# Scan stage of an eight-stage kernel: where the expert mix and the product delta · xs are computed

## The reference

```python
xc = _silu(xc + conv_b[None, :, None])               # after a causal convolution with 4 taps
dt_lo, Bm, Cm = ...                                  # three slices of x_ld @ x_proj_w.T
delta = jax.nn.softplus(dt_lo @ dt_proj_w.T + dt_proj_b)
def step(h, inp):                                    # h: 512 channels x 16 states
    dA = jnp.exp(d_t[:, :, None] * negA[None])
    h = dA * h + (d_t * x_t)[:, :, None] * B_t[:, None, :]
    y_t = jnp.einsum('bdn,bn->bd', h, C_t)
y = (y + x_ld * D[None, None, :]) * _silu(z_bld)
out = y @ out_proj_w.T
```

## Time and profile before

| | before |
|---|---|
| runs | 2511.66, 2512.00, 2514.43 us; median 2512.0 |
| profiled execution | 2519.74 us, its span 2518.0 us |
| scan stage, first scan to end of the last | 1255.3 to 1758.6 us |
| PE, DVE, ACT, POOL busy over the span | 88, 66, 58, 35 per cent |
| mean granted PE clock | 0.938 of full speed |

### The profile page before, as it was taken

One profiled execution on the slowest core, in us unless ns is written; L12 is line 12 of the kernel. 1 busy time (PEld: TensorE's weight loads), 2 busy tenths in 40 slices (PEclk: granted clock), 3 DMA queues, 4 the chain that ended last, 5 costly groups with the idle time before them and its releaser, 6 DMA issues. The chain is left out here.

```text
span 2518.0 us, 47690 instructions
## 1 busy us (share of the span) xinstructions
PE 2217.8 (88%) x16425; PEld 1937.2 (77%) x16425; DVE 1674.2 (66%) x4020; ACT 1453.1 (58%) x3815; POOL 889.7 (35%) x906
## 2 busy tenths in 40 slices
PE   6887979999999979998489999999686899996997
PEld 4776968999999959997266676677685576766997
DVE  5785767888888846554498898777464554554554
ACT  5674547777777723333487777775342566663342
POOL 3221240011111120000678887667485233332000
PEclk8897989999999979999699999999897999997999
DMA  4000120000000463333311111000400000000001
GB/s 151 1 1 17 35 68 18 2 18 18 18 18 18 144 197 119 120 111 94 129 41 51 51 50 47 35 35 1 119 1 1 1 1 1 1 1 1 1 1 34
DMA packets 74371, 111.77 MB, mean 44 GB/s; under 512 B 16174, under 2 KB 59814, under 8 KB 73016
## 3 DMA queue, kind: packets, MB, share of 16 engines
q1 hardware_dynamic: 66648, 87.23, 10.7%
q0 software_dynamic: 7488, 21.50, 2.6%
HBM read 79.73 MB, written 28.97 MB: 43 GB/s over the span
## 5 line engine op out<-in xcount | busy, mean ns | idle before, releaser
L2064 POOL TENSOR_TENSOR l2a_hb<-l2a_hb,l2a_Cb 128x1024 f32<-128x1024 f32 x128 | 302.8, 2377 | 107.7 <-DVE l2a_hb L2551 106.5
L2551 DVE TENSOR_TENSOR_SCAN l2a_hb<-l2a_dA,l2a_dB 128x1024 f32<-128x1024 f32 x128 | 288.8, 2275 | 31.4 <-PE l2a_dB L2158 26.1
L2158 PE MATMUL l2a_dB<-l2a_diag,l2a_dxT 64*128 64x128 f32 x2048 | 190.1, 306 | 38.8 <-DVE l2a_hb L2551 25.9
L2158 PEld LDWEIGHTS l2a_dB<-l2a_diag,l2a_dxT 64*128 64x128 f32 x2048 | 139.9, 194 | 104.0 <-PE l2a_dB L2158 37.2
L2388 ACT ACTIVATE l2a_dA<-l2a_delta,l2a_An 128x255 f32<-128x255 f32 x512 | 213.4, 498 | 6.9 <-DVE l2a_hb L2551 6.7
L964 PE MATMUL l1a_QK<-l1a_xh,early_wqkv_h 128*128 128x256 f32 x512 | 147.1, 287 | 1.5 <-DVE l1a_xl L128 1.5
L964 PE MATMUL l1a_QK<-l1a_xh,early_wqkv 128*128 128x256 f32 x512 | 144.6, 282 | 0.0
L964 PE MATMUL l1a_QK<-l1a_xl,early_wqkv_h 128*128 128x256 f32 x512 | 144.3, 282 | 0.0
L2178 PE MATMUL l2a_YS<-ident,l2a_hb 128*128 128x128 f32 x1024 | 142.2, 285 | 1.0 <-POOL l2a_hb L2064 1.0
L1240 ACT ACTIVATE l1a_ex<-l1a_S,l1a_nm 128x256 f32<-128x256 f32 x256 | 119.3, 471 | 36.5 <-DVE l1a_nm L1292 35.1
L2178 PEld LDWEIGHTS l2a_YS<-ident,l2a_hb 128*128 128x128 f32 x1024 | 116.5, 145 | 12.2 <-POOL l2a_hb L2064 1.3
(11 more groups left out here) (767 smaller groups left out, 7812.4 us busy)
## 6 DMA issues: line engine op xcount, KB each, us to landing
l2a_Cb<-c_rows SPq DMA_DIRECT2D x8, 2048.0 KB
l1f_xl<-moe_x_rows SPq DMA_DIRECT2D x95, 128.0 KB
moe_y_rows<-l1f_yo SPq DMA_DIRECT2D x95, 128.0 KB, 1.7
first_raw<-in_L_attn_w_qkv_dram SPq DMA_DIRECT2D x18, 256.0 KB, 2.8
moe_x_rows<-X SPq DMA_DIRECT2D x1, 4224.0 KB, 17.2
l1f_dL<-in_L_ffn_Wd_dram SPq DMA_DIRECT2D x1, 3072.0 KB
X<-in_L_attn_x_dram SPq DMA_DIRECT2D x8, 256.0 KB, 6.0
routes_raw<-in_L_attn_w_o_dram SPq DMA_DIRECT2D x4, 512.0 KB
```

Of the source, the lines that this page charges most:

```text
L2064: nc.gpsimd.tensor_tensor(h[:, :, :], h[:, :, :], Cb[p][:, s0:s0 + UN, :], ALU.mult).then_inc(hc_ready, 1)
L2158: last = nc.tensor.matmul(out[:, m:m + 2, j * P + a:j * P + a + HP], dxT[q][a:a + HP, j, c * P:(c + 1) * P], diag[q][a:a + HP, j, s0 + m:s ...
L2551: nc.vector.tensor_tensor_scan(flat(hb[u % RING]), flat(dA[(i * NU + u) % DAS]), dB[u % 2][:, :], 0.0, ALU.mult, ALU.add).then_inc(scanned, 1)
```

## The change

The mix of items 3 to 7 leaves DVE. ACT multiplies the four gathered rows of a half by their weights, in place, in four instructions (`act_scale`, half 0 at unit 10, half 1 at unit 11). POOL adds: rows 0 and 1 to rows 2 and 3 (512 elements), the two sums (256), and X (256), each waiting for the one before (`pool_mix`, after its product of units 11 and 12). DVE keeps mean and variance, now after scan 13 (`dve_mix_stats`); POOL's scale and shift follow its product of unit 14, and ACT's normalisation stands at unit 15, ahead of the tap of the next convolution. All four gathers of half 0 are issued at units 12 to 15.

The sum delta is written over the logarithm in PSUM; DVE multiplies it there by xs into dx, in two halves, and ACT copies delta to SBUF at unit 11 (`act_keep_delta`). PE's turn of x and of dx, and the exponentials of the next item, wait for that copy (`delta_kept`).

```diff
@@ -1894,8 +1894,8 @@
-    SECOND_HALF, FIRST_HALF = (0, 1, 2, 3), (5, 6, 13, 14)
-    MIX = {3: (0, (0, 1)), 4: (0, (2, 3)), 5: (1, (0, 1)), 6: (1, (2, 3))}
+    SECOND_HALF, FIRST_HALF = (0, 1, 2, 3), (12, 13, 14, 15)
+    SCALE_AT, ADD_AT, STATS_AT, MIXED_AT = 10, 11, 13, 15
...
@@ -1996,10 +1998,6 @@
-        def pool_dx(pool, k, q):
-            pool.wait_ge(delta_ready, k + 1)
-            nc.gpsimd.tensor_tensor(dx[:, :, :], delta[q][:, :, :], xs[:, :, :], ALU.mult).then_inc(dx_ready, 1)
...
@@ -2008,6 +2006,17 @@
+        def pool_mix(pool, k, j):
+            pool.wait_ge(m_scaled, ((k - 3) * NT + j + 1) * TOPK)
+            nc.gpsimd.tensor_tensor(my[j][:, 0:2, :], my[j][:, 0:2, :], my[j][:, 2:4, :], ALU.add).then_inc(m_summed, 1)
+            if j == 0:
+                pool.wait_ge(m_done, k * NT)
+            pool.wait_ge(m_summed, (k * NT + j) * TOPK + 1)
+            nc.gpsimd.tensor_tensor(mr[:, j, :], my[j][:, 0, :], my[j][:, 1, :], ALU.add).then_inc(m_summed, 1)
+            pool.wait_ge(m_summed, (k * NT + j) * TOPK + 2)
+            nc.gpsimd.tensor_tensor(mr[:, j, :], mr[:, j, :], sh.X[:, k, j], ALU.add).then_inc(m_summed, 2)
...
@@ -2070,14 +2079,14 @@
                         pool_diag(pool, i + 1, 1 - p, 1)
-                    if u == 10 and ahead:
-                        pool_dx(pool, i + 1, 1 - p)
+                    if u in (ADD_AT, ADD_AT + 1) and i + 3 < ITEMS:
+                        pool_mix(pool, i + 3, u - ADD_AT)
+                    if u == STATS_AT + 1 and i + 3 < ITEMS:
+                        pool_rstd(pool, i + 3)
                     if u in SECOND_HALF and not first and i + 3 < ITEMS:
                         pool_gather(pool, i + 4, 0, FIRST_HALF.index(u))
-                    if u == 8 and i + 3 < ITEMS:
-                        pool_rstd(pool, i + 3)
...
@@ -2107,7 +2116,7 @@
         def pe_turn_x(pe, i):
-            pe.wait_ge(delta_ready, i + 2)
+            pe.wait_ge(delta_kept, (i + 2) * 2)
             turn(ph, pe, i + 2, F[1])
...
@@ -2135,7 +2144,8 @@
         def pe_dx(pe, k):
-            pe.wait_ge(dx_ready, k + 1)
+            pe.wait_ge(dx_ready, (k + 1) * 2)
+            pe.wait_ge(delta_kept, (k + 1) * 2)
             for j in range(NT):
...
@@ -2326,6 +2336,12 @@
+        def act_keep_delta(act, k, q):
+            for h in range(2):
+                act.wait_ge(dx_ready, k * 2 + h + 1)
+                nc.scalar.copy(pair_of(delta[q], h), F[h][:, :] if k else ln0[h]).then_inc(delta_kept, 1)
...
@@ -2351,6 +2367,13 @@
+        def act_scale(act, k, j):
+            act.wait_ge(half_in[j], 16 * TOPK * (k - 1))
+            for n in range(TOPK):
+                nc.scalar.activation(my[j][:, n, :], my[j][:, n, :], ACT.Copy,
+                                     scale=sh.moe_wk[:, k * NT + j, n:n + 1]).then_inc(m_scaled, 1)
...
@@ -2381,7 +2404,9 @@
                 if u == 0:
-                    act.wait_ge(delta_ready, i + 1)
+                    if i == 0:
+                        act_keep_delta(act, 0, q)
+                    act.wait_ge(delta_kept, (i + 1) * 2)
                 if i * NU + u >= DAS:
...
@@ -2400,6 +2425,8 @@
                 for u in range(NU):
+                    if u == 11 and ahead:
+                        act_keep_delta(act, k, q)
                     if u + LEAD < NU:
...
@@ -2427,7 +2454,9 @@
                         act_out(act, i - 1)
-                    if u == 12 and i + 3 < ITEMS:
+                    if u in (SCALE_AT, SCALE_AT + 1) and i + 3 < ITEMS:
+                        act_scale(act, i + 3, u - SCALE_AT)
+                    if u == MIXED_AT and i + 3 < ITEMS:
                         act_mixed(act, i + 3)
...
@@ -2476,8 +2505,12 @@
-                last = nc.vector.tensor_tensor(pair_of(delta[q], h), pair_of(delta[q], h), F[h][:, :] if k else ln0[h], ALU.add)
-            last.then_inc(delta_ready, 1)
+                ln = F[h][:, :] if k else ln0[h]
+                nc.vector.tensor_tensor(ln, pair_of(delta[q], h), ln, ALU.add).then_inc(delta_ready, 1)
+            dve.wait_ge(xs_ready, (k + 1) * FC)
+            for h in range(2):
+                dve.wait_ge(delta_ready, k * 2 + h + 1)
+                nc.vector.tensor_tensor(pair_of(dx, h), F[h][:, :] if k else ln0[h], pair_of(xs, h), ALU.mult).then_inc(dx_ready, 1)
...
@@ -2494,21 +2527,21 @@
-            if j == NT - 1 and terms[-1] == TOPK - 1:
-                for h in range(NT):
-                    dve.wait_ge(m_summed, (k * NT + h + 1) * TOPK)
-                    nc.vector.bn_stats(m_st[:, h, :], mr[:, h, :]).then_inc(m_stats_ready, 1)
-                dve.wait_ge(m_stats_ready, (k + 1) * NT)
-                nc.vector.memset(ph.carrier[:, :], 0.0)
-                for h in range(NT):
-                    nc.vector.bn_aggr(m_mv[:, h, :], m_st[:, h, :]).then_inc(m_var_ready, 1)
-        def dve_dx(dve, q):
-            dve.wait_ge(delta_ready, 1)
-            for h in range(2):
-                last = nc.vector.tensor_tensor(pair_of(dx, h), pair_of(delta[q], h), pair_of(xs, h), ALU.mult)
-            last.then_inc(dx_ready, 1)
+            if j == NT - 1:
+                dve_mix_stats(dve, k)
+        def dve_mix_stats(dve, k):
+            for h in range(NT):
+                dve.wait_ge(m_summed, (k * NT + h + 1) * TOPK)
+                nc.vector.bn_stats(m_st[:, h, :], mr[:, h, :]).then_inc(m_stats_ready, 1)
+            dve.wait_ge(m_stats_ready, (k + 1) * NT)
+            nc.vector.memset(ph.carrier[:, :], 0.0)
+            for h in range(NT):
+                nc.vector.bn_aggr(m_mv[:, h, :], m_st[:, h, :]).then_inc(m_var_ready, 1)
+        def dve_keep_dx(dve, q):
...
@@ -2560,8 +2593,8 @@
                         dve_delta(dve, i + 1, 1 - p)
-                    if u in MIX and i + 3 < ITEMS:
-                        dve_mix(dve, i + 3, *MIX[u])
+                    if u == STATS_AT and i + 3 < ITEMS:
+                        dve_mix_stats(dve, i + 3)
                     if u == 6 and not first:
                     if u == 15 and ahead == 2:
```

More of the change, by code:

```diff
@@ L1913, in l2_attn @@
                                       for k, n in enumerate(("shift_ready", "m_shift_ready")))
+        m_scaled = ctx.enter_context(nc.semaphore("l2a_m_scaled", num=PHASE_SEMS.stop + 7))
+        delta_kept = ctx.enter_context(nc.semaphore("l2a_delta_kept", num=QUANT_SEMS.stop))
         wi_loaded = ctx.enter_context(nc.semaphore("l2a_wi_loaded", num=POOL_DMA_SEMS.stop))
@@ L2283, in act_silu @@
         def act_silu(act, k):
-            act.wait_ge(dx_ready, k)
+            act.wait_ge(dx_ready, k * 2)
             if k:
@@ L2529, in _ @@
             dve_delta(dve, 0, 0)
-            dve_dx(dve, 0)
+            dve_keep_dx(dve, 0)
             def gate(k, q):
```

## The result

Measured beside the kernel before: 2559.4 us against 2511.8 (medians of four runs each), ratio 1.0186, interval 1.0168 to 1.0204. The forecast was 2554, within 2538 to 2572. Five more runs on another chip gave 2556.3 against 2512.4, ratio 1.0180 (1.0166 to 1.0193). The profiled execution took 2560.3 us, span 2558.6.

The account below looks back on a forecast made before the run. The prediction took PE to bound the front half and a chain over all engines the back half, where POOL's queue would decide. Losses of 37.9, 2.4 and 1.8 us made +42, so 2512.0 would become 2554 us, range 2538 to 2572.

Parts of the forecast that it names:

- Front half is PE's, gain nothing: First scan to scan 7: PE is the bound, so taking the mix's 9.7 us per item off DVE gains 0.
- the rival of relief: Front half: if it hung on DVE, the mix would return 48.3 us, giving 2474 us; chance 0.05.
- dx on DVE, +1.2: Back half, ahead of scan 11: two products of 0.60 us each, unhidden, in all seven items that prepare a next one.
- POOL's queue, 19.1 us: End of scan 11 to the shift: products, additions (2.9 a half), gathers, scale and shift without a pause; chance 0.78.
- The stop before the statistics: After scan 13: DVE stands some 6 us for POOL's second half of additions, without lengthening POOL's queue.
- the normalisation does: Ahead of the tap: ACT waits 6.4 us for POOL's shift; the next item's scan 0 starts 9.9 us later.
- The sum, +42: Whole kernel: 37.9 us in items 0 to 4, 2.4 in items 5 and 6, 1.8 at the start.
- the start's 1.8: Before the first scan: ACT's table load and first exponentials wait for DVE's products and the copy, +1.8 us.
- the 1.9 that PE's slack takes back: Next item's start: scan 0 comes 9.9 us later, but PE's dB of unit 3 only 8.0 later.
- the clock: Item starts: PE idles, adding a low-clock stretch per item, 3.5 us in five items, 18 in all: 2572 us; chance 0.10.
- Item 5 "near 66": Sign that the forecast is right: item 5 near 66 us long, beside items 1 to 3 near 73.
- POOL is in time: Back half: additions cost almost nothing, ACT's queue sets the end, +1.5 us per item, 2524 us; chance 0.06.

Follow-up runs that it names:

- e7: Kernel before, with the mix of items 3 to 7 left at its first of four terms (part of the computation omitted): 2509.5 us, ratio 1.0006.
- e1: Only delta's part of the change (delta in PSUM, dx on DVE, ACT's copies), the mix as in the kernel before: 2521.4 us, ratio 1.0048.
- e8: Full change with the mix's statistics on DVE behind scan 15 instead of scan 13: 2554.1 us, ratio 1.0171 against the kernel before.
- e3: Full change with ACT's normalisation moved behind both taps, at unit 0 of the next item: 2536.3 us, ratio 1.0108 against the kernel before.
- e2: Only the mix's part of the change, dx staying on POOL as in the kernel before: 2555.9 us, ratio 1.0183.
- e5: Full change with half 0's four gathers issued behind the scale and shift, at units 14 and 15: 2546.2 us, ratio 1.0138 against the kernel before.
- e4: Full change with statistics, scale and shift, normalisation and staging moved into the next item (units 1, 3, 4, 6): 2528.5 us, ratio 1.0075 against the kernel before.

## Why the prediction was right, and where its sizes were off

**Front half is PE's, gain nothing: right.** In item 1 from PE's dB of unit 3 to DVE's residual: 1328.52 to 1350.97 before, 1334.32 to 1356.78 after, 22.45 and 22.46 us, with eight multiply-additions less between. e7 shows it by experiment, and rules out the rival of relief. The argument was made on items 4 and 5 and does not hold for the front half of item 0, where the change shortened the stretch from scan 3 to scan 7 from 22.0 to 17.9 us; that the gain was lost again by scan 11 (3.1 us behind the kernel before, where the forecast had 3.0) was not reckoned and is luck for the forecast.

**dx on DVE, +1.2: right.** e1 has 1.2 in items 1, 2, 4, 5 and 6; item 3, which had a longer low-clock stretch before, shows 0.2.

**POOL's queue, 19.1 us: right.** 19.2 from scan 11's end to the shift's. The additions of a half came to 3.0 with their hand-offs (1379.98 to 1382.94), where 2.9 was taken from POOL's rows of other stages.

**The stop before the statistics does not count, the normalisation does: right.** DVE stood 1.10 + 4.80 us (forecast some 6), e8 shows that it costs nothing while the other wait is there. ACT waited 7.09 us (forecast 6.4); e3 gives back two fifths of the loss with that one move.

**The sum, +42 against +47.5 (and +45 in the second measurement).** By items, from first scan to first scan, profile against profile, the forecast in the same form in brackets (its first term with the start's 1.8, and the 1.9 that PE's slack takes back set where the next item starts): +12.7 (12.5), +8.2 (8.0), +9.8 (8.0), +8.9 (7.0), +8.0 (6.1), -0.6 (-0.7), +1.2 (1.2), -1.5 (0): 46.8 against 42.1. Items 0, 1, 5 and 6 are right to 0.2; the last item had a stretch at low clock before and has none after. Items 2, 3 and 4 are 1.8 to 1.9 too short in the forecast, and all three have the low-clock stretch in their fronts. So the term mis-sized is the clock. I had it as a rival of 18 us (3.5 in each of five items) that either comes or doesn't, and at nothing in the forecast's sum. In fact it came in three items at 1.6 each, and in one in the second profile. The same step of 1.6 shows between items of like work within e2 (75.74 with the stretch, 74.10 without) and e5 (73.37 and 71.73), and e8's item 5, with one, is 65.5 us long where the full change's is 63.95. That it is the stretch at 0.5 and not something that goes with it is read from rows of four kernels; no run changed the clock alone.

**Item 5 "near 66": wrong.** It is 63.95. I named the length for that check without the 1.9 us that the item before hands back at its start; the sum had it right.

**The rival "POOL is in time"** did not come, since POOL's queue was as long as forecast. e4 comes near to what it describes, no wait for POOL, though its normalisation stands elsewhere: it is 19 us slower than the kernel before where the rival had 12, so that work, placed there, has a price without any wait for POOL.

The Trainium skill ("GPSIMD Engine Reference", section "8. Key points") has DVE about twice as fast as GpSimd in elementwise work; here dx took 1.2 us on DVE and 2.3 on POOL, which agrees. The rule only says what a move costs the engine that receives it, and not who waits for that engine.

## What to carry to other kernels

A busy engine need not be the bound: compare two stretches of the same loop with and without the work in question, and if they are equally long, moving it gains nothing there (and look at the first round of the loop too, which can have another bound). Then the only question is what the receiving engine's queue does to those who wait behind it: list everything that it issues between its last free moment and the value that another engine needs, and add it up. And where several engines wait for one late queue, the waits hide each other: taking one away shows the next (here ACT's normalisation, then DVE's statistics, then PE's sums), so reckon the room of each before moving anything.

## What was not expected of the hardware

DVE's multiply-additions of 128x256, both inputs in SBUF, lasted from 453 to 3144 ns in the kernel before, median 768, with POOL's products running beside them, against a mean of 513 before the stage, and none of it reached the time (e7: ratio 1.0006). With them gone, POOL's products went from 2377 to 2364 ns, 1.7 us over all 128. These rows agree with the collision that the Trainium skill describes ("SBUF — State Buffer", section "SBUF: two separate sides"). No run separated it from other causes; whatever it was, it made DVE's instructions longer, POOL's hardly, and cost the kernel nothing.

What a stretch at the lower clock goes with depends on where it falls: 3.4 us at 0.5 beginning some 8 us after an item's first scan, where PE is the bound, went with 1.6 us more; the same within the first microsecond of items 2 and 4 of the second profile of the full change with nothing. In e3, where no normalisation stands ahead of the tap, items with such a stretch just before or across their start (1, 2 and 4) are 1.5 to 1.7 us longer up to the end of scan 3 than item 3. In the back half of the kernel before every item has one of 3.4 us; item 3 has 6.8 us, up to 50.4 us after its start, and is 1.0 longer than its neighbours (66.33 us against 65.37). In e1 the items with 6.8 us of it, up to 49.8 us after their start, are as long as those with 3.4 (66.57 and 66.56).
